# A 3x3 box convolution on one Trainium2 core: columns innermost, high halves read in place

## What is computed

```python
def _ln_c(v, eps=1e-06):
    m = jnp.mean(v, axis=1, keepdims=True)
    s = jnp.var(v, axis=1, keepdims=True)
    return (v - m) / jnp.sqrt(s + eps)
...
x = x + conv3x3(_ln_c(x), kernel=1/9)              # per channel
t = tokens(x)                                      # (B, H*W, C)
t = t + ffn(_ln_t(t), Wa, ba, Ws, bs)              # changes features 64..87 alone, else the identity
x = from_tokens(t)
```

## Time and profile before

| | us |
|---|---|
| median of 3 runs | 826.19 (824.92 to 826.85) |
| span of the profiled execution | 823.9 |
| DVE busy | 728.5 (88%) |
| PE busy | 543.2 (66%) |
| ACT busy | 490.5 (60%) |
| POOL busy | 441.7 (54%) |
| DMA, 68.02 MB | 71.4% of 16 engines' span in the main queue |
| mean granted clock of TensorE | 0.899 |

### The profile page before, as it was taken

One profiled execution on the slowest core, in us unless ns is written; L12 is line 12 of the kernel. 1 busy time (PEld: TensorE's weight loads), 2 busy tenths in 40 slices (PEclk: granted clock), 3 DMA queues, 4 the chain that ended last, 5 costly groups with the idle time before them and its releaser, 6 DMA issues. The chain is left out here.

```text
span 823.9 us, 10762 instructions
## 1 busy us (share of the span) xinstructions
PE 543.2 (66%) x2258; PEld 241.8 (29%) x2295; DVE 728.5 (88%) x1479; ACT 490.5 (60%) x739; POOL 441.7 (54%) x708
## 2 busy tenths in 40 slices
PE   0024678876776777668676777767677677788760
PEld 0001233333332333333323233333333323333330
DVE  1739999999999999969999999979999999999540
ACT  0101577766766666657666666667666666678940
POOL 0203766656566656535666665645666565666500
PEclk9966688999889899979999899979989989989995
DMA  9599980594159907892069906660039009769999
GB/s 106 52 146 196 193 140 1 65 172 71 27 77 158 150 1 103 100 172 37 7 96 143 163 0 97 84 77 0 7 44 147 7 0 88 40 48 55 68 85 77
DMA packets 626042, 68.02 MB, mean 83 GB/s; under 512 B 625856, under 2 KB 625984, under 8 KB 625984
## 3 DMA queue, kind: packets, MB, share of 16 engines
q1 hardware_dynamic: 625984, 67.46, 71.4%
HBM read 33.90 MB, written 33.55 MB: 82 GB/s over the span
## 5 line engine op out<-in xcount | busy, mean ns | idle before, releaser
L799 ACT ACTIVATE xbuf<-xbuf,shift,gain (+1 forms) x256 | 222.7, 937 | 0.0
L556 DVE TENSOR_SCALAR n<-xbuf,mean,rn 128x256 f32 (+1 forms) x256 | 218.0, 886 | 0.0
L671 POOL TENSOR_TENSOR nlo<-n,nhi 128x1024 f16<-128x1024 f32 x64 | 137.1, 2142 | 132.1 <-ACT nhi L782 132.1
L782 ACT ACTIVATE nhi<-n 128x1024 f16<-128x1024 f32 x64 | 67.7, 1057 | 234.9 <-DVE n L556 234.9
L565 DVE BATCH_NORM_STATS2 stat<-xbuf 128x6 f32 (+1 forms) x256 | 173.7, 682 | 19.3 <-DMA xbuf<-x 19.3
L582 DVE TENSOR_TENSOR xbuf<-ps,xbuf 128x512 f32 (+1 forms) x128 | 164.2, 1282 | 16.7 <-DMA xbuf<-x 14.4
L839 PE MATMUL ps<-nhi,band 128*128 128x512 f16 (+1 forms) x408 | 121.8, 418 | 26.4 <-DVE xbuf L582 15.1
L878 PE MATMUL ps<-h1m,w2m 128*128 128x512 f32 x256 | 134.2, 606 | 0.0
L680 POOL TENSOR_TENSOR ut<-xbuf,mean 128x536 f32<-128x536 f32 x32 | 44.3, 1385 | 146.9 <-DVE shift L485 146.9
L839 PE MATMUL ps<-nlo,band 128*128 128x512 f16 (+1 forms) x408 | 115.0, 398 | 0.0
L881 PE MATMUL ps<-h1lo,w2r 128*128 128x512 f32 x128 | 58.5, 457 | 74.3 <-DVE h1lo L596 73.6
(11 more groups left out here) (94 smaller groups left out, 763.3 us busy)
## 6 DMA issues: line engine op xcount, KB each, us to landing
xbuf<-x SPq DMA_DIRECT2D x16, 1024.0 KB, 11.6
out<-xbuf SPq DMA_DIRECT2D x32, 512.0 KB, 7.1
xbuf<-x SPq DMA_DIRECT2D x30, 512.0 KB, 6.9
out<-xbuf SPq DMA_DIRECT2D x12, 1024.0 KB, 12.7
out<-xbuf SPq DMA_DIRECT2D x16, 256.0 KB, 8.0
xbuf<-x SPq DMA_DIRECT2D x4, 256.0 KB, 6.7
consts<-cst SPq DMA_DIRECT2D x1, 170.0 KB, 2.4
h<-ws SPq DMA_DIRECT2D x8, 10.0 KB
```

The costliest lines, as they stand in the source:

```text
L556: ins = v.tensor_scalar(n32[:, w // HALF, w % HALF, :], xview(par)[:, jc * CW + w, :], mean[:, k, w:w + 1], rn[:, k, w:w + 1], ALU.subtrac ...
L671: pool.tensor_tensor(nlo[:, at:at + HALF, :], n32[:, h, :, :], nhi[:, at:at + HALF, :], ALU.subtract).then_inc(lo_ready, 1)
L782: act.activation(nhi[:, at:at + HALF, :], n32[:, s, :, :], ACT.Copy).then_inc(hi_ready, 1)
L799: ins = act.activation(col, col, ACT.Identity, bias=shift[:, k, w:w + 1], scale=gain[:, k, w:w + 1])
```

## The change

The convolution no longer works on the normalised x but on x times rstd/9, because a mean that is the same for all channels of a pixel drops out of what follows: the second norm takes it away, and the output's shift becomes mean(x) - gain x mean(x1). The scaled x goes as f32 into `z`, [channel][18 columns], a ring of two windows of eight columns with a column of halo on each side. PE reads the upper 16 bits of each f32 in `z` in place as bf16, with a step of two. POOL writes the rest, z minus that bf16, as f32r into `zlow`. A chunk is now cut into four quarters of 64 channels with all eight columns, no longer into pairs of columns.

- DVE: `normalise` (eight) goes; `scale(q)` comes, a tensor_tensor of x and the broadcast `rx`, four a step, on chunk t-2. `add_convolution` works on quarters, the statistics of x1 come after all four of them. put(0) moves to the top of the step; the sequence of the step is new. gm and shift are one operation more.
- POOL: four `low(q)` of 64 x 10 elements, of chunk t-2; two ahead of ut, two behind u.
- ACT: the copy to nhi goes; in every other step a copy of two columns of all channels carries the halo to the start of `z`. Its output now waits for `fin_ready`.
- PE: `convolve` stands at the end of each group in place of its start, waits for low(q), and has three bf16 and three f32r matmuls of 512 columns.
- Short edits: `mean` is set to zero once, ut and g lose their own buffers, `rx_ready`, `z_ready` and `halo_ready` replace `n_ready` and `hi_ready`.

```diff
+        z = sb("z", [P, C, ZW], F32)
+        zlow = sb("zlow", [P, C, CW + 2], F32R)
...
+        def zhigh(jc, q, lo, n):
+            at = 2 * (window(jc) + lo) + 1
+            return z[:, :, :].bitcast(BF16)[:, q * QC:(q + 1) * QC, at:at + 2 * n - 1:2]
...
+                elif i == 4:
+                    at = (j - 1) % CHUNKS * CW
+                    v.tensor_scalar(rx[:, at:at + CW], rstd[:, k, 0:CW], 1.0 / 9.0, None,
+                                    ALU.mult).then_inc(rx_ready, 1)
+                    lnc.count(v.tensor_scalar(gain[:, k, :], rstd[:, k, CW:], 1.0, None, ALU.add))
+                elif i == 5:
+                    lnc.count(v.tensor_tensor(gm[:, :], gain[:, k, :], mean[:, k, CW:], ALU.mult))
                     lnc.end()
                 else:
-                    v.tensor_scalar(rn[:, k, :], rstd[:, k, 0:CW], SCALE / 9.0, None, ALU.mult)
-                    v.tensor_scalar(gain[:, k, :], rstd[:, k, CW:], 1.0, None, ALU.add)
-                    v.scalar_tensor_tensor(shift[:, k, :], mean[:, k, CW:], -1.0, rstd[:, k, CW:],
-                                           ALU.mult, ALU.mult).then_inc(fin_ready, 1)
+                    v.tensor_tensor(shift[:, k, :], mean[:, (j - 3) % 4, 0:CW], gm[:, :],
+                                    ALU.subtract).then_inc(fin_ready, 1)
...
-                def normalise(w):
...
-                        ins = v.tensor_scalar(n32[:, w // HALF, w % HALF, :], xview(par)[:, jc * CW + w, :],
-                                              mean[:, k, w:w + 1], rn[:, k, w:w + 1], ALU.subtract, ALU.mult)
...
+                def scale(q):
+                    if conv:
+                        c, jc, par = conv
+                        at = window(jc)
+                        if q == 0:
+                            v.wait_ge(rx_ready, t)
+                        wait(v, conv_done, 4 * c + q - 3)
...
+                        v.tensor_tensor(z[:, q * QC:(q + 1) * QC, to:to + hi - lo], quarter(par, q, (lo, hi)),
+                                        over(rx[:, lo:hi].unsqueeze(1), [P, QC, hi - lo]),
+                                        ALU.mult).then_inc(z_ready, 1)
...
+                        part = quarter(par, s, (jc * CW, jc * CW + CW))
                         v.wait_ge(conv_done, 4 * c + s + 1)
+                        v.tensor_tensor(part, ps[:, B_CONV + s % 2, :].rearrange("p (c w) -> p c w", w=CW),
+                                        part, ALU.add).then_inc(x1_done, 1)
```

The new order of DVE's step behind `low_parts(0)` and `finish(0)`, and of POOL's, PE's and ACT's new parts:

```diff
+                put(0)
                 finish(1)
                 x_statistics(0)
                 finish(2)
+                put(1)
                 finish(3)
+                put(2)
                 finish(4)
+                scale(0)
                 x_statistics(1)
+                finish(5)
+                put(3)
+                scale(1)
+                x_statistics(2)
+                finish(6)
+                put(4)
+                scale(2)
+                counted = x_statistics(3)
+                put(5)
+                scale(3)
+                add_convolution(0)
+                low_parts(2)
+                add_convolution(1)
+                put(6)
+                add_convolution(2)
+                put(7)
+                add_convolution(3)
+                wait_x1()
+                put(8)
                 x1_statistics(0)
                 x1_statistics(1)
                 if tok:
                     v.wait_ge(rank_ready, tok[0] + 1)
                     v.tensor_reduce(mx1[:, :, :], gw[:, :, :, :], mybir.AxisListType.X,
                                     ALU.max).then_inc(top_ready, 1)
+                x1_statistics(2)
                 counted = x1_statistics(3) or counted
...
+                def low(q):
+                    if conv:
+                        c, jc, par = conv
+                        pool.wait_ge(z_ready, 4 * c + q + 1)
+                        if q == 0 and jc % 2 == 0 and jc > 0:
+                            pool.wait_ge(halo_ready, halos(c, jc))
+                        pool.tensor_tensor(zlow[:, q * QC:(q + 1) * QC, :], zparts(jc, q), zhigh(jc, q, 0, CW + 2),
+                                           ALU.subtract).then_inc(lo_ready, 1)
+                low(0)
+                low(1)
...
+                low(2)
+                low(3)
...
+                if conv and conv[1] % 2 == 0 and conv[1] > 0:
+                    c = conv[0]
+                    act.wait_ge(z_ready, 4 * c)
+                    act.activation(z[:, :, 0:2], z[:, :, 2 * CW:2 * CW + 2], ACT.Copy).then_inc(halo_ready, 1)
...
                 wait(pe, x1_done, 4 * c + s - 1)
+                pe.wait_ge(lo_ready, 4 * c + s + 1)
+                for d in (1, 0, 2):
+                    pe.matmul(bank, band[:, :], zhigh(jc, s, d, CW), start=d == 1, stop=False)
+                for d in (0, 1, 2):
+                    ins = pe.matmul(bank, bandr[:, :], zlow[:, s * QC:(s + 1) * QC, d:d + CW], start=False, stop=d == 2)
                 ins.then_inc(conv_done, 1)
...
                 for s in range(GROUPS):
-                    if conv:
-                        convolve(conv, s)
...
                         ins.then_inc(ft_done, 1)
+                    if conv:
+                        convolve(conv, s)
```

More of the change, by code:

```diff
@@ L22 @@
 HALF = CW // 2
-RING = 16
+QUARTERS = 4
+QC = C // QUARTERS
+ZW = 2 * CW + 2
 GROUPS = CW // 2
@@ L233, in build @@
         fin_ready = sem("fin_ready")
[L234 to L235 removed]
+        rx_ready = sem("rx_ready")
+        z_ready = sem("z_ready")
+        halo_ready = sem("halo_ready")
         lo_ready = sem("lo_ready")
@@ L662, in step @@
             def step(t, j, pair):
-                norm = chunk_at(t, j, pair, 1)
+                conv = chunk_at(t, j, pair, 2)
                 tok = chunk_at(t, j, pair, 3)
                 k4 = (j - 3) % 4
[L667 to L671, removed]
-                                       ALU.subtract).then_inc(lo_ready, 1)
+                def low(q):
[8 more added lines that the diff above has]
+                low(1)
                 if tok:
@@ L776, in step @@
                                        ACT.Copy).then_inc(ft_copied, 1)
-                    if norm and s < 2:
-                        c, jc, par = norm
-                        at = (jc * CW + s * HALF) % RING
-                        act.wait_ge(n_ready, 2 * c + s + 1)
-                        wait(act, conv_done, 2 * (2 * c + s) - 5)
-                        act.activation(nhi[:, at:at + HALF, :], n32[:, s, :, :], ACT.Copy).then_inc(hi_ready, 1)
                     if s == 3 and (not known(t) or t <= NCHUNK + 1):
@@ L822, in convolve @@
                 c, jc, par = conv
-                w = jc * CW + 2 * s
-                bank = ps[:, B_CONV + s % 2, :].rearrange("p (w c) -> p w c", w=2)
-                pieces = []
-                for d in (0, -1, 1):
-                    if 0 <= w + d and w + d + 2 <= W and (w + d) % RING != RING - 1:
-                        pieces.append((0, 2, (w + d) % RING))
-                    else:
-                        pieces += [(i, 1, (w + d + i) % RING) for i in range(2) if 0 <= w + d + i < W]
-                wait(pe, x1_done, 4 * c + s - 1)
-                if s in (0, 1, 3):
-                    pe.wait_ge(lo_ready, 2 * c + (1 if s == 0 else 2 if s == 1 or jc == CHUNKS - 1 else 3))
-                n = 0
-                for src in (nhi, nlo):
-                    for i, k, at in pieces:
-                        n += 1
-                        ins = pe.matmul(bank[:, i:i + k, :], band[:, :], src[:, at:at + k, :],
-                                        start=n == 1, stop=n == 2 * len(pieces))
+                bank = ps[:, B_CONV + s % 2, :].rearrange("p (c w) -> p c w", w=CW)
+                wait(pe, x1_done, 4 * c + s - 1)
+                pe.wait_ge(lo_ready, 4 * c + s + 1)
[3 more added lines that the diff above has]
+                    ins = pe.matmul(bank, bandr[:, :], zlow[:, s * QC:(s + 1) * QC, d:d + CW], start=False, stop=d == 2)
                 ins.then_inc(conv_done, 1)
@@ L926, in constants @@
     near = (np.abs(rows[:, None] - rows[None, :]) <= 1) & (rows[:, None] // H == rows[None, :] // H)
-    k[:, K_BAND:K_BAND + P] = near / SCALE
+    k[:, K_BAND:K_BAND + P] = near
     k[:, K_RANK:K_RANK + 3 * NIB] = np.tile(NIB - np.arange(NIB), 3)
```

88 lines of the change are left out of this document (33 added, 55 removed).

## The result

The changed kernel takes **947.76 us** (median of 4 runs, 947.13 to 948.75) against 826.52 (4 runs, 824.92 to 828.63) measured beside it: a ratio of **1.1465, 95% interval 1.1444 to 1.1485**. Slower was forecast, but 121 us are about twice the 60 of the sum, and the time lies above the range. The profiled execution has a span of 946.9 us and a mean granted clock of 0.825, before 0.899.

A forecast was written before the change was run, and what follows sets the result against it. DVE, busy 88%, was taken to bound the kernel before; the new ring takes 24.4 us a step against 22.5, 51 us over 27 steps, plus 9 for step 33: together +60, 886 us, range 805 to 935.

The forecast's parts named there:

- (1): Top of the step: put(0) makes DVE stand 1.2 us at the read of ya; scale(0) runs 3.85 to 4.53.
- (2): Scales on DVE alternate with low parts on POOL, each waiting for the other; scale(3) runs 12.5 to 13.2.
- The rival that POOL does not stop a tensor_tensor: DVE scales with a broadcast input run beside POOL; PE's queue is the ring, 22.1 us a step, 822 us; chance 0.25.
- a waiter is held to POOL's recorded end: Five DVE/POOL waits in (2) each end 0.29 us later: step 25.8 us, time 925; chance 0.06.
- (4): End of the step: addition 3 to 21.4, then four statistics and the maximum, reaching 24.4 us.
- The slow-run rival: Eight-column runs on DVE as slow as single columns, 1.28 us: 28.0 us a step, 987; shares chance 0.16.
- the signs that the prediction named for being right: DVE share well below 88%, waits at additions 2, 3 and ya; scales over 1.2 us; PE's h1lo wait longest.
- A side sum: DVE's own work, without waits for other engines, falls from 22.5 to about 14.5 us a step.
- step (3): Group 2: PE waits for the middle h1lo, done at 14.4, its remaining step queued behind; conv(3) ends at 20.7 us.
- the prediction's first rival: The faster one: POOL does not stop DVE's scales, PE's own queue sets 22.1 us a step, 822 us; chance 0.25.
- The quarter: Six convolution matmuls on PE take 1.31 us; strided high halves cost nothing, at most 0.65 us a quarter.
- The rival of the clock: PE's clock falls in a gap before conv(2) each step: 2.4 us, 903 to 950; shares chance 0.16.

The follow-up runs named there:

- the warm run: Dummy matmuls added to the changed kernel in PE's two gaps, 14 before the wait for the top h1lo and 12 before the wait for low(0): 892.7 us.
- second block of rows of the quarters: PE timeline of the changed kernel with the low part as bf16 in place of f32r, multiplied with the bf16 band: 933.0 us.

## Why the prediction was right in sign and wrong in size

**Right.** (1) The wait at ya, unseen before and taken from the chain's rows, is there: 1.50 us, 1.2 forecast. It comes 2.98 us after s_var, forecast 2.12. Half of the rest is the lower clock (transposes start to ya 1.20, 0.79 forecast), half is s_var itself, which takes 0.63 where it took 0.17 before: POOL's feat runs under it. (2) Scales and low parts alternate as forecast: low parts 1.25 (1.40 forecast), scale(2) held by ut to 1.87, addition 0 at 12.84 after s_var (13.1), the middle h1lo done at 14.1 (14.4). That the sum is so close is in part luck: scale(0) starts 1.2 later than forecast (5.06, 3.85), and scale(3) makes up for it, since it does not wait for low(2) but starts 0.04 ahead of it (499.62, 499.66). The rival that POOL does not stop a tensor_tensor is out. So is the one that a waiter is held to POOL's recorded end: scale(2) ends at 498.48, and less the 0.69 of a free one it started at 497.79, while ut's record ends at 497.92. It is 0.13 ahead, not the 0.29 that the prediction read from the normalisation (its own rows of hot and nlo give 0.15), so the rule of the Trainium skill ("SBUF — State Buffer", section "SBUF: two separate sides") is nearer to the row than the prediction had it. (4) From addition 3 to the next s_var: 3.96 us, forecast 3.7. The slow-run rival (additions at 1.28) is out, at 0.69. Of the signs that the prediction named for being right, one did not come: one scale of four takes over 1.2 us in the step read, not all. Another came by another way: in the loop PE's wait for h1lo stays its longest (3.83 us in the step read), but it is the h1lo at the top of the step, not the middle one on which the sum rests. A side sum is off by 0.9: 22.5 less the 7.1 that its terms give is 15.4 us of DVE work, not 14.5; the time does not hang on it.

**Wrong: step (3),** "PE itself is there by 12.2, or by 14 at the lower clock, so it waits for DVE and not the other way round." PE takes the middle h1lo 16.05 us after s_var, 3.85 later than the 12.2. The rows above give its parts: conv(0) starts 1.11 later (7.14 in place of 6.03, by the later top); conv(0) and the tile take 5.61 (494.52 to 500.13), in the warm run 3.75 (492.83 to 496.58), so 1.86 is the clock; and two quarters are dearer by 0.43 each, 0.86. Together 3.83. (The split between the first two parts is that of this step: in the 19 long steps conv(0) starts 6.4 to 7.4 us after s_var and conv(1) 12.3 to 12.8, and an earlier conv(0) does not bring an earlier conv(1).) The first 2.2 of it are hidden behind h1lo (12.2 to 14.4), the other 1.65 are not. Behind h1lo come two more quarters, +0.83 to addition 3, and +0.26 at the end. That makes 24.4 + 1.65 + 0.83 + 0.26 = 27.1, the step that was read (487.38 to 514.52). The ring that set the step is thus the one of the prediction's first rival, PE's own queue from low(0) to conv(3), which it tied to a POOL that stops nobody and priced at 22.1 us. At the measured prices it gives the same 27.1: conv(0) at 7.14, four quarters of 1.74, 6.9 for the tile work between, 1.86 for the clock, 0.3 for the last one's end, and 3.96 to the next s_var.

So two terms of the sum were mis-sized. **The quarter** was taken at 1.31 and measured 1.74: the prediction took adjacent-column prices for reads with a step, on the argument that the same bytes are fetched, and gave runs of eight in f32r no price at all. The first was known as a bound (0.65) and set to its lower end; 0.23 was measured. **The clock**: it was listed as a rival, worth 2.4 us a step, with the gap in the wrong place (ahead of conv(2)). The gap that decides lies ahead of low(0) and the top h1lo, where the forecast's own times give PE nothing to do, and the row at 425.60 showed that PE comes out of a gap at 0.50. It belonged in the sum; by the warm run it is worth 2.0 us a step, 55 us, where 62 were missed. The savings do not simply add: with the clock up, the quarters ahead of h1lo are hidden again. The rival of the clock was given 903 to 950, and that this holds the 948 is partly luck, since its gap was another and the price of the quarters was not in it. The range stopped at 935, at two dear terms, and here three came together: the step of two, the runs of eight and the clock.

## What to carry to other kernels

When work that lay one step apart is put into one step, sum the ring over all engines, each with its queue in its order, and lay out where each engine stands idle: here PE's idle stretches of 3.83 and 3.45 us were followed by work at a granted clock of 0.50, and that cost more than any one dear instruction (55 us against 25 and 16). A queue's order counts as much as its work: a read whose result nobody needs soon should stand behind the instruction that starts the ring. An order that shows nothing alone, as low(2) first did, may still count once another wait is gone, so test it together with the others before you drop it, and once without it.

## What the runs showed of the hardware

- Three bf16 matmuls of 512 columns that read every second element in runs of eight take 0.90 us at full clock, 0.70 if the eight are adjacent (same run, second block of rows of the quarters). The Trainium skill ("Advanced Engine Details and Errata", section "SBUF Cachelines") says that at least two hits on a line of 16 bytes are needed to hide the access. Here a run of eight spans 32 bytes, so its reads fall on two or three lines, up to four on one, and 0.07 us a matmul is paid all the same; whether a line at the end of a run is hit only once, no run shows.
- f32r matmuls on 64 runs of eight cost 0.04 us each more than on 512 adjacent elements (0.13 for three).
- A DVE operation of 0.17 us (s_var) took 0.63, and two of 0.15 at the least (gm, shift) 0.83 and 0.82, with a POOL operation under them: here short operations with two SBUF inputs are held like long ones.
